# A decoder layer with a mixture of experts: the shared expert in groups of four tiles with its first two weights held still

## The reference

```python
def _swiglu(x, wg, wu, wd):
    return jax.nn.silu(x @ wg) * (x @ wu) @ wd          # 256 -> 512 -> 256

xf = x.reshape(-1, H)                                   # 4096 tokens, H = 256
...                                                     # norm, logits, softmax
tk_probs, tk_idx = jax.lax.top_k(probs, TOP_K)          # TOP_K = 2 of 8
...
out = _swiglu(xf, sWg, sWu, sWd)                        # the shared expert, every token
for e in range(NUM_EXPERTS):
    out = out + w[:, e:e + 1] * _swiglu(xf, Wg[e], Wu[e], Wd[e])
```

## Time and profile before

| what | value |
|---|---|
| median of three executions | 1781.2 us (1780.03 to 1785.51) |
| the profiled execution | 1781.99 us |
| its span, first to last instruction | 1780.3 us |
| mean granted TensorE clock | 0.979 of full speed |
| busy over the span: PE, DVE, ACT, POOL | 1694.7, 1386.3, 1112.4, 360.2 us |
| share of the last product of this part (L1741) in the chain that ended last | 9% of the span |
| moved by DMA | 120.43 MB, 68 GB/s in the mean |

### The profile page before, as it was taken

One profiled execution on the slowest core, in us unless ns is written; L12 is line 12 of the kernel. 1 busy time (PEld: TensorE's weight loads), 2 busy tenths in 40 slices (PEclk: granted clock), 3 DMA queues, 4 the chain that ended last, 5 costly groups with the idle time before them and its releaser, 6 DMA issues. The chain is left out here.

```text
span 1780.3 us, 36372 instructions
## 1 busy us (share of the span) xinstructions
PE 1694.7 (95%) x11950; PEld 1108.4 (62%) x11951; DVE 1386.3 (78%) x2651; ACT 1112.4 (62%) x2304; POOL 360.2 (20%) x431
## 2 busy tenths in 40 slices
PE   6899999999999999979889999997899999999998
PEld 3343333333333333356568999985798888888887
DVE  5699999999999999433678899984658666666663
ACT  4338888888888888912467888883226555544552
POOL 2100000000000000050043222221120455555540
PEclk9969999999999999999999999998999999999999
DMA  5702211111111220063211221114515233333335
GB/s 192 207 10 40 35 33 30 30 29 29 30 30 30 40 40 8 24 192 87 114 43 34 91 84 34 33 34 150 170 57 169 48 53 53 53 53 53 51 55 160
DMA packets 95823, 120.43 MB, mean 68 GB/s; under 512 B 18987, under 2 KB 76639, under 8 KB 94591
## 3 DMA queue, kind: packets, MB, share of 16 engines
q1 hardware_dynamic: 77936, 95.15, 19.3%
q0 software_dynamic: 13728, 18.88, 6.4%
q10 hardware_dynamic: 4047, 4.91, 0.9%
HBM read 71.25 MB, written 42.40 MB: 64 GB/s over the span
## 5 line engine op out<-in xcount | busy, mean ns | idle before, releaser
L506 DVE TENSOR_REDUCE half_max<-psA 128x1 f32<-128x512 f32 x1024 | 632.9, 683 | 9.9 <-PE psA L559 8.6
L538 ACT ACTIVATE PT<-psB 128x1024 f32<-128x1024 f32 x512 | 518.2, 1025 | 121.4 <-PE psB L569 121.2
L559 PE MATMUL psA<-KS,QS 48*128 48x512 f32 x1024 | 397.1, 466 | 4.1 <-PEq L104 2.0
L569 PE MATMUL psB<-QS,KS 50*128 50x512 f32 x1024 | 365.3, 454 | 0.2 <-ACT PT L538 0.2
L588 PE MATMUL psO<-PT,VG 128*32 128x256 f32 x4096 | 327.2, 392 | 4.5 <-ACT OU L528 0.4
L559 PEld LDWEIGHTS psA<-KS,QS 48*128 48x128 f32 x1024 | 162.8, 190 | 221.6 <-DVE half_max L506 162.6
L588 PEld LDWEIGHTS psO<-PT,VG 128*32 128x32 f32 x4096 | 82.0, 108 | 191.9 <-issue 114.2
L1741 PE MATMUL m_psY<-swd_high,m_hT 128*128 128x256 f32 x824 | 173.1, 293 | 12.7 <-DVE m_hT L1876 9.3
L1346 ACT ACTIVATE x_probs<-x_scores,x_neg_max 128x77 f32<-128x77 f32 x512 | 176.3, 358 | 3.4 <-DVE x_neg_max L1252 3.2
L569 PEld LDWEIGHTS psB<-QS,KS 50*128 50x128 f32 x1024 | 145.2, 186 | 13.1 <-ACT PT L538 10.5
L1741 PEld LDWEIGHTS m_psY<-swd_high,m_hT 128*128 128x128 f32 x824 | 134.2, 189 | 23.3 <-DVE m_hT L1876 12.4
(11 more groups left out here) (213 smaller groups left out, 2746.4 us busy)
## 6 DMA issues: line engine op xcount, KB each, us to landing
QS<-q_parts SPq DMA_DIRECT2D x96, 128.0 KB
q_parts<-part SPq DMA_DIRECT2D x16, 512.0 KB, 3.8
OT<-OU SPq DMA_DIRECT2D x32, 256.0 KB, 2.7
mx_kept<-cx_mx SPq DMA_DIRECT2D x4, 1232.0 KB, 10.1
cx_mx<-mx_kept SPq DMA_DIRECT2D x4, 1232.0 KB, 7.0
KS<-k_parts SPq DMA_DIRECT2D x32, 128.0 KB
xf_rows<-XF SPq DMA_DIRECT2D x32, 128.0 KB, 1.7
acc<-X SPq DMA_DIRECT2D x32, 128.0 KB, 1.8
```

Of the source, the lines that this page charges most:

```text
L506: dve.tensor_reduce(half_max[:, h * (TB // 2) + t % (TB // 2), n:n + 1], psA[:, bank_of(slot, 2 * v + r), :], axis=AX.X, op=ALU.max).then_ ...
L538: act.activation(PT[:, k % 4, 2 * a:2 * a + 2, :].rearrange("p h n -> p (h n)"), psB[:, u % 2, :, :].rearrange("p a n -> p (a n)"), ACT.Ex ...
L559: pe.matmul(psA[:, bank_of(slot, m), :], QS[top:top + KQ, slot, h // 2, t * P:(t + 1) * P], KS[top:top + KQ, slot, n * HALF:(n + 1) * HALF ...
L569: mm = pe.matmul(psB[:, u % 2, r, :], KS[top:top + KM, slot, c * P:(c + 1) * P], QS[top:top + KM, slot, a, half * HALF:(half + 1) * HALF], ...
```

## The change

The shared expert's tiles are taken in groups of four ("quads"), six early and two late; the expert tiles keep the old pipeline. In a quad, a step is no longer a tile of tokens but a chunk of 128 of the 512 inner values. Four tiles of tokens are turned ahead into one place of 512 columns (`xq`). For chunk j the 128 columns j of a first weight are held in the array and the 512 tokens pass, so that the hidden values come out with the inner values on the partitions, as the last product wants them; the four transposes of the hidden values are gone. ScalarE's high part and VectorE's low part of the hidden values read SBUF (`SG`) instead of PSUM. The last product of chunk j adds 3 matmuls of 256 columns for each of the four tiles to four sums in PSUM (`psY` and `psH`, two each), which VectorE takes in together at the end of the quad: three before the first gate of the next quad, the fourth after its first low half.

The next quad's tiles are turned in the fourth step: two before that step's low half, two after it. The very first quad is turned before anything else. `beside(s)` stays at the end of a step. SP issues by quads: four stores with four loads of sums, then the weights of four steps in one block, then the loads of four tiles. The last expert's third weight is loaded after the last early product, since `xq` lies on its place. The late tiles' sums come in one load of 1 MB, and the six copies to the output go out right behind it.

```diff
+            def hidden(i, j):
+                pe.wait_ge(t_in, i - j + QUAD)
+                for n, (bank, done, read) in enumerate(((psG, g_done, silu_done), (psU, u_done, h_done))):
+                    if i >= 2:
+                        pe.wait_ge(read, i - 1)
+                    for k in range(KD):
+                        for a, b in PRODUCTS:
+                            mm = pe.matmul(bank[:, i % 2, :], SHARED[n][b][:, k, j * P:(j + 1) * P], xq[a][:, k, :],
...
+            def last(i, j, tiles):
+                if tiles[0] == 0:
+                    pe.wait_ge(ht_in, i + 1)
+                    if j == 0:
+                        if i:
+                            pe.wait_ge(y_in, i)
+                        if i == END:
+                            pe.wait_ge(swd_in, 32)
+                for q in tiles:
+                    for a, b in PRODUCTS:
+                        mm = pe.matmul(bank_of(q), whole(HL[a][:, i % 2, :, :])[:, of_quad(q)], SHARED[2][b][:, j, :],
...
+            def quad(i0, ahead):                       # TensorE
+                for j in range(KF):
+                    i = i0 + j
+                    hidden(i, j)
+                    if j == KF - 1:
+                        turn_ahead(ahead, (0, 1))
+                    if j:
+                        last(i - 1, j - 1, range(QUAD))
+                    if j == KF - 1:
+                        last(i, j, range(1))
+                        turn_ahead(ahead, (2, 3))
+                        last(i, j, range(1, QUAD))
+                    beside(i)
...
+            def quad(i0, before, ahead):               # VectorE
+                for j in range(KF):
+                    i = i0 + j
+                    if j == 0 and before is not None:
+                        take_in(before, range(QUAD - 1))
+                    gated(i, i % 2)
+                    if j == KF - 1:
+                        turned_ahead(ahead, (0, 1))
+                    low(i)
+                    if j == 0 and before is not None:
+                        take_in(before, range(QUAD - 1, QUAD))
+                    if j == KF - 1:
+                        turned_ahead(ahead, (2, 3))
+                    beside(i)
...
+            def quad(i0, ahead):                       # ScalarE
+                for j in range(KF):
+                    i = i0 + j
+                    act.wait_ge(g_done, i + 1)
+                    if i >= 2:
+                        act.wait_ge(ht_in, i - 1)
+                    act.activation(SG[:, i % 2, :], psG[:, i % 2, :], ACT.Silu).then_inc(silu_done, 1)
+                    if j == KF - 1:
+                        turned_ahead(ahead, (0, 1))
+                    act.wait_ge(h_done, i + 1)
...
+                    act.activation(whole(HL[0][:, i % 2, :, :]), SG[:, i % 2, :], ACT.Copy).then_inc(ht_high, 1)
+                    if j == KF - 1:
+                        turned_ahead(ahead, (2, 3))
+                    beside(i)
...
-                            mm = pe.matmul(psY[:, e_bank, 0:D], HL[a][:, e, k, :], SHARED[2][b][:, k, :],
```

More of the change, by code:

```diff
@@ L1489, in phase_ffn @@
         slot = table("r_slot", A3)
+        routed = place[0]
         slot_of = table("r_slot_of", [P, NT, TOP])
@@ L1547, in has_parts, with bank_of, turned_bank, of_quad @@
             return not isinstance(i, int) or EARLY_TILES <= i + 1 < END
[L1549 to L1552, removed]
+        QUADS = [QUAD * c for c in range(EARLY_TILES // QUAD)] + [END + QUAD * c for c in range(LATE // QUAD)]
+        assert EARLY_TILES % QUAD == 0 and LATE % QUAD == 0 and KF == QUAD
+        def bank_of(q):
+            return (psY if q < 2 else psH)[:, 0, q % 2 * D:(q % 2 + 1) * D]
+        def turned_bank(i, q):
+            return psG[:, (i - q) % 2, 0:D] if q % 2 else psT[:, 0, 0:D]
+        def of_quad(q):
+            return slice(q * P, (q + 1) * P)
+        def whole(ap):
+            return ap.rearrange("p k n -> p (k n)")
+        def experts(t):
+            return t if t and not shared(t[0]) else None
+        def steps(step, eng):
+            for s in range(EARLY_TILES + 1, EARLY_TILES + 4):
+                step(lambda lag, s=s: (s - lag, (s - lag) % 2))
             with eng.Fori(EARLY_TILES // 2 + 2, END // 2) as j:
@@ L1687, in step @@
             def step(tile):
-                if tile(1) and not shared(tile(1)[0]):
-                    if peeled(tile(1)[0], EARLY_TILES + 1):
+                if t := experts(tile(1)):
+                    if peeled(t[0], EARLY_TILES + 1):
                         pe.wait_ge(slots_done, 5)
-                    expert = expert_of(tile(1)[0])
-                if t := tile(2):
+                    expert = expert_of(t[0])
+                if t := experts(tile(2)):
                     i, e = t
@@ L1760, in beside @@
                     mm.then_inc(inverted, 1)
-            steps(step, pe, beside)
+            turn_ahead(0, range(QUAD))
+            for i0 in QUADS:
+                if i0 == END:
+                    steps(step, pe)
+                quad(i0, i0 + QUAD)
         @block.vector
@@ L1907, in step @@
                         dve.tensor_tensor(SHARED[2][1][:, :, :], WD[:, x, :, :], SHARED[2][0][:, :, :], ALU.subtract).then_inc(wd_low, 1)
+                if (t := tile(0)) and not experts(t):
+                    dve.wait_ge(wd_low, NTM)
+                    for q in range(2 * (t[0] - END), 2 * (t[0] - END) + 2):
+                        turned_tokens(END + q, q)
             chain = route()
@@ L1965, in beside @@
                         act.wait_ge(w_in, 16 * 2 * NE)
-                    for w, high, low in SPLIT:
+                    for w, high, small in SPLIT:
                         act.activation(high[:, x, :, :], w[:, x, :, :], ACT.Copy).then_inc(w_high, 1)
-            steps(step, act, beside)
+            turned_ahead(0, range(QUAD))
+            for i0 in QUADS:
+                if i0 == END:
+                    steps(step, act)
+                quad(i0, i0 + QUAD)
 def decoder_layer(nc, T):
```

268 lines of the change are left out of this document (181 added, 87 removed).

## The result

The change took 1805.97 us in the median of four executions (1802.78 to 1808.94), the kernel before 1783.36 in the median of four (1780.03 to 1788.59): a ratio of 1.0124, 95% interval 1.0091 to 1.0157. The direction is the one forecast; the size, forecast as 1794 with a range up to 1804, is too small.

What follows compares the result with a forecast made beforehand. The prediction took VectorE's chain to bound the early stretches after the change. Its terms, 6.1 to tile 16's product, 5.0 splits, 1.0 into the experts, 0.9 late tiles, added 13.0 to 1782.0, giving 1794 against the median of 1781.2; range 1784 to 1804.

Steps and rivals of the forecast that it cites:

- splits: From tile 16's product to the first expert product, where routed experts' weights are split: 43.6 us, before 38.6, so +5.0.
- The step that failed: Low clock after TensorE's five waits of 3 to 5 us: at most some 8, taken as nothing beside VectorE's chain.
- The loop of step 3: Fourth step of a group: low half, three matmuls, turning of tiles 2 and 3, back to VectorE; about 2.0, twice.
- the wait for TensorE behind it: In the routing steps, VectorE waits once for TensorE's count matmuls and next product: 2.4 us.
- The clock rule: TensorE's clock follows how busy its array was recently; by that rule the sum moves up, towards 1800.
- The function table: ScalarE's table loads around Exp: 1.28 us each; a drain of some 1.4 per switch would make the sum 2.8 higher.
- Into the experts: TensorE's second expert product starts 5.9 us after the first instead of 4.9, VectorE waiting for the last sum: +1.0.
- Late tiles: The shared expert's last 8 tiles: -1.3 from the work, +2.2 from token rows queued behind copies, so +0.9 us.
- The seam: Passage from expert tiles to late tiles: the shared product starts 7.0 us after tile 93's last product, before 0.4.
- (a): Rival: TensorE stays the bound in all stretches, so the kernel gets faster, 1770 us; chance 0.08.
- (b): Rival: about even, as the queue, the fourth step's loop and the ring's waits hide, 1785 us; chance 0.14.
- (c): Rival: HBM-to-HBM copies run at half the full queue's rate, 9.4 longer; with half the clock's 8, 1807 us; chance 0.10.

Runs made afterwards that it cites:

- e1: The change with matmuls that belong to nothing put where TensorE waits, so that it does not stand still; 1803.01 us, ratio 1.0096 to the kernel before.
- e2: The change with the weights of steps 4 to 7 and the six output copies queued behind the token rows; 1799.06 us, ratio 1.0082.
- e7: The change with later weights and copies, tiles turned before the fourth step's last product, side work between gate and low half, early Exp; 1789.86 us, ratio 1.0034.

## Why the prediction came out too low

- **Start, queue, slot steps, splits: about right.** The start cost 2.6, 2.3 and 2.6 (forecast 2.0); the idle before a low half is 0.70 (0.65); VectorE stood 3.81 in step 7, 1.9 more than in step 3, for the late rows (2.0); the slot steps took 51.9 (51.6), the splits 43.1 (43.6), a split step 4.61 (4.73).
- **The step that failed:** "They cost nothing where VectorE is the chain anyway ... I take nothing, because they lie where VectorE is the chain." The chain passes over TensorE in just these places. After the wait in a fourth step VectorE needs the turnings of tiles 2 and 3, the end of the last product to take it in, and the next product for its gate, and in step 3 most of these ran at the low level. e1 shows the price: 3.9 up to the first expert product, 6.7 to the end (means of the change less e1). That is most of the 7.6 by which the mean end lies behind the forecast's. The bound named beside the step, some 8, was nearer than nothing.
- **Two terms of the routing came out by luck.** The loop of step 3 was priced at 2.0 and measured 1.94, the wait for TensorE behind it at 2.4 and measured 3.44 (0.20 and 3.24); but both were measured with TensorE at the low level for most of the time (grant 0.56). With TensorE kept busy (e1) they are 1.35 and 1.75, so for the clock that the forecast assumed they were 1.3 too large together. Against that, VectorE's second gate came 14.9 after the first turning, forecast 14.1, in e1 as in the change. That e1's marks lie so near the forecast's owes something to errors that cancel.
- **The range.** The forecast stands on 1781.2 for the kernel before; with its fourth execution the median is 1783.4, so 2.2 of the 12.0 by which 1794 was too low are not the change's. The change's own executions lie on both sides of 1804.
- **The clock rule** that the prediction weighed moved the sum the right way: the grant is lower in just the stretches in which TensorE's busy share fell (0.89, 0.94 and 0.90). The Trainium skill (TensorE: Matmul & The Clock Gate, Part 1: The HAM clock gate) says that the clock is set by how busy the array has been recently; the grants agree.
- **The function table.** ScalarE's timeline shows 0.02 between the Exp and the load and 0.01 between the load, 1.28 long, and the next Silu. The Trainium skill (ScalarE: Activation LUTs, What ACT_TABLE_LOAD costs) adds a drain of some 1.4 us to each switch; the trace has no room for it:

```profile
1243.92 0.42 ACT L2173 ACTIVATE r_ex<-r_ex 128x256 f32<-128x256 f32 x1 [0.24 <-DVE r_ex L1907]
1244.36 1.28 ACT L2128 ACT_TABLE_LOAD   x1
1245.65 0.60 ACT L2128 ACTIVATE m_silu<-m_psG 128x512 f32<-128x512 f32 x1
```

- **Into the experts** 6.7, 5.4 and 6.2 (5.9): where the clock holds it is 5.5 (e1), 0.4 less than the term.
- **Late tiles.** The seam was priced without its clock: in the three profiles it is 8.2, 7.6 and 8.1 from tile 93's end to the shared product (7.0), with TensorE kept busy (e1) 7.1. In the first profile that moved the load of the sums and the copies to 13.5 and 13.9 (12.9), and the rows of tile 101, which land behind them, to 28.1 (26.2); the product behind that wait ran at the low level (grant 0.69). Hence 54.6 from tile 93's end, forecast 50.1.
- **The rivals.** (a) and (b) fell. (c) came nearest in time, 1807, but 9.4 of the 13.4 that it adds rest on the wrong cause: the sums, the copies and the rows, 4.5 MB, had landed 14.7 after the first of them was sent (1766.09 to TensorE's turning at 1780.77), 304 GB/s, not half of 334. Its other 4, for the clock, had the right cause and were too few (6.7).

The turnings of the hidden values are gone as forecast (a late step is 4.18, e.g. 1767.84 to 1772.02, before 4.86), but this paid only where TensorE was the bound, in the last tiles, and there the seam ate it: in e2 the seam takes 8.1 and the rest 40.8, before 0.4 and 48.8.

## What to carry to other kernels

In this kernel a wait on TensorE, such as the 4.52 us of step 3, could cost twice: once itself, and once in what TensorE did next at the low clock (2.3 there). Before that is counted as nothing, follow the chain on from the wait and look whether it passes over TensorE within the next products. And a product that is made cheaper by grouping tiles can give up the overlap between tiles, as it did here; look first at what the other engines were doing in it.

## What the runs showed of the hardware

Between 100 and 200 us, in attention, the granted clock was 0.75 to 0.90 from one execution to another of kernels that are the same there, and the first turning came at 1223.7 to 1239.1. Effects of 5 us had to be read from stretches behind it.

One of VectorE's eight one-hot tables took 2.07 in e7, where it began while GpSimd multiplied; the other seven took 1.22. First VectorE's timeline, then GpSimd's:

```profile
1283.36 1.22 DVE L1986 TENSOR_TENSOR r_hot_row<-r_row_no,r_slot_row 128x1024 f32<-128x1024 f32 x1
...
1286.75 2.07 DVE L1986 TENSOR_TENSOR r_hot_row<-r_row_no,r_slot_row 128x1024 f32<-128x1024 f32 x1
```

```profile
1286.61 1.14 POOL L1729 TENSOR_TENSOR r_hot_tile<-r_hot_tile,r_token 128x568 f32<-128x568 f32 x1
```

The long one ended 1.07 after GpSimd's instruction, about as if it had begun only then. The Trainium skill (SBUF — State Buffer, Terms) says that the two engines share a pair of ports which one holds for a whole instruction; the two rows agree.
